# A graph network's set-up: the features' load goes to GpSimd's queue, their largest value is taken earlier, and the verdict goes ahead of the scales

## The reference, cut to what matters

```python
edge_index = jnp.stack([src, dst])
x = _layernorm(x + _L0_gnn_ref(x, edge_index, Wl, bl, Wr, ln_w, ln_b))   # 4 layers: mean over neighbours, two matmuls, layernorm, relu
x = _layernorm(x + _L1_gnn_ref(x, edge_index, edge_weight, W, b))        # sum over neighbours of a linear map
x = _layernorm(x + _L2_gnn_ref(x, src, dst, Wq, Wk, Wv, Wo, ...))        # attention over the edges, batch norms, feed-forward
x = _layernorm(x + _L3_gnn_ref(x, edge_index, W, b))                     # mean over neighbours and a linear map
```

## Time and profile before

| | us |
|---|---|
| three runs | 1333.36, 1333.84, 1334.45 (median 1333.84) |
| the profiled execution | 1335.18 |
| its span, first to last instruction | 1333.2 |
| end of ScalarE's pass over x, last work of the set-up | 51.96 |
| mean granted TensorE clock, as a share of full speed | 0.833 |
| busy: TensorE / VectorE / ScalarE / GpSimd | 990.6 / 867.2 / 523.6 / 413.0 |

### The profile page before, as it was taken

How to read it: one execution, slowest core, us unless ns; L and a number is a source line. 1 busy time by engine, 2 the same in 40 slices (tenths; PEclk the granted TensorE clock), 3 DMA queues, 4 the chain that set the end, 5 groups by cost and what they waited for, 6 DMA issues and landing times. The chain is left out here.

```text
span 1333.2 us, 18242 instructions
## 1 busy us (share of the span) xinstructions
PE 990.6 (74%) x6074; PEld 622.3 (47%) x6074; DVE 867.2 (65%) x2126; ACT 523.6 (39%) x1007; POOL 413.0 (31%) x516
## 2 busy tenths in 40 slices
PE   1289989999999998894655565656656565557997
PEld 1168845645556454454433343434434333345554
DVE  4879946734434467466377877777877777764343
ACT  1289913111111111112456555556655556424210
POOL 4000000000000000001277777777777777720000
PEclk9999999999999999896865766666666766568999
DMA  6000061000000000000543333333333333319000
GB/s 156 26 1 1 1 211 34 1 9 0 9 1 0 17 16 23 12 1 24 154 123 104 106 106 104 106 105 106 107 105 106 107 105 105 107 44 226 12 24 26
DMA packets 49496, 87.78 MB, mean 66 GB/s; under 512 B 12384, under 2 KB 35315, under 8 KB 49161
## 3 DMA queue, kind: packets, MB, share of 16 engines
q0 software_dynamic: 20608, 55.20, 14.4%
q1 hardware_dynamic: 26312, 29.89, 8.3%
q10 hardware_dynamic: 2492, 1.61, 0.5%
HBM read 70.68 MB, written 15.98 MB: 65 GB/s over the span
## 5 line engine op out<-in xcount | busy, mean ns | idle before, releaser
L1413 POOL DMA_INDIRECT counts_all<-kv_d,counts_all x416 | 394.4, 948 | 154.7 <-issue 145.9
L867 PE MATMUL bank<-counts_all,parts 125*128 (+2 forms) x1750 | 344.4, 355 | 19.5 <-DVE parts L1047 9.7
L867 PEld LDWEIGHTS bank<-counts_all,parts 125*128 125x128 f16 x1750 | 159.8, 98 | 190.9 <-DVE parts L1047 11.0
L1553 PE MATMUL bank<-counts_all 125*128 125x128 f16 x1230 | 133.9, 288 | 83.3 <-ACT counts_all L1619 82.9
L1299 POOL IOTA iota_n<- 128x256 f16 x1 | 0.3, 349 | 562.1 <-POOLq L854 562.1
L1553 PEld LDWEIGHTS bank<-counts_all 125*128 125x128 f16 x1230 | 110.1, 133 | 126.6 <-ACT counts_all L1619 126.3
L1542 PE MATMUL bank<-rel_rows,ident_h 104*128 104x512 f16 x104 | 56.9, 547 | 124.6 <-ACT away L1609 123.9
L1483 DVE TENSOR_TENSOR counts_all<-counts_all,bank 128x512 f32<-128x512 f32 x104 | 71.5, 687 | 117.6 <-DMA counts_all<-kv_d,counts_all 117.6
L1568 PE MATMUL bank<-counts_all,parts 128*128 128x272 f16 x615 | 135.2, 378 | 14.3 <-DVE counts_all L1461 12.1
L670 PE MATMUL bank<-parts 128*125 128x125 f16 x625 | 102.7, 324 | 12.0 <-DVE parts L589 12.0
L1609 ACT ACTIVATE away<-bank,lane_bias 125x512 f16<-125x512 f32 x173 | 110.8, 680 | 1.0 <-PE bank L1542 0.7
(11 more groups left out here) (268 smaller groups left out, 1264.2 us busy)
## 6 DMA issues: line engine op xcount, KB each, us to landing
counts_d<-counts_all SPq DMA_DIRECT2D x1, 6835.9 KB
counts_all<-counts_d SPq DMA_DIRECT2D x1, 6835.9 KB
counts_all<-kv_d,counts_all POOLq DMA_INDIRECT x416
kv_d<-counts_all SPq DMA_DIRECT2D x6, 448.0 KB
q_d<-counts_all SPq DMA_DIRECT2D x1, 1562.5 KB
x<-in_x SPq DMA_DIRECT2D x6, 250.0 KB
out<-parts SPq DMA_DIRECT2D x6, 250.0 KB
inv_deg<-in_x SPq DMA_DIRECT2D x1, 1400.0 KB
```

The costliest lines, as they stand in the source:

```text
L867: last = T.matmul(agg_ps[p][:, 0:w], pin[:, s, part, :], counts[:, s, bass.ds(b * BLK, w)], start=(s + part == 0), stop=(s + part == NT))
L1413: G.indirect_dma_start(out=out_rows, out_offset=None, in_=table_d, in_offset=bass.IndirectOffsetOnAxis(ap=index, axis=0)).then_inc(signal, 16)
L1553: last = T.matmul(pick_ps[n % DEEP][:, k * C:(k + 1) * C], ohT[n % DEEP][:, tile - GTILES[n][0], k, :], Q[:, tile, part, :], start=(tile = ...
```

## The change

- SP no longer loads x. GpSimd issues the same two DMAs, behind all its constants and behind waits for both edge lists, and ahead of its five gathers.
- VectorE takes the largest feature (lines 401 to 404) right behind the chunk starts, ahead of the limits.
- VectorE's verdict, with its wait for `edge_ok_summed`, goes ahead of the copy of the largest feature (line 446) and so ahead of `alpha`. The scaled identities stay behind `alpha`.

TensorE's and ScalarE's lists are as they were.

```diff
--- before.py
+++ after.py
@@ -273,9 +273,6 @@
                     load_rows(sp, dst_rows, dst, dst_in)
                     sp.wait_ge(code_ready, 1)
                     sp.dma_start(code_d[:, 0:LANES].rearrange("(g r) p -> r g p", r=ROWS), code[:, :, :]).then_inc(code_out, 16)
-                    x_tiles = x.rearrange("(t p) c -> p t c", p=TILE)
-                    for rows in SPRAY:
-                        sp.dma_start(xf[rows, :, :], x_tiles[rows, :, :]).then_inc(x_in, 16)
                     sp.wait_ge(dstN_ready, 1)
                     sp.dma_start(dstf_d, dstN[:, :]).then_inc(setup_out, 16)
                     sp.wait_ge(srci_ready, 1)
@@ -338,6 +335,12 @@
                     last.then_inc(limits_ready, 1)
                     iota(iota_kp[:, :, :].rearrange("p (s d) w -> p s d w", d=WN), [[1, NT], [NT, WN], [0, BATCH]], 0, 0)
                     iota(iota_tp[:, :, :], [[1, TILE], [0, BATCH]], 0, 0)
+
+                    pool.wait_ge(dst_in, 48)
+                    pool.wait_ge(src_in, 48)
+                    x_tiles = x.rearrange("(t p) c -> p t c", p=TILE)
+                    for rows in SPRAY:
+                        pool.dma_start(xf[rows, :, :], x_tiles[rows, :, :]).then_inc(x_in, 16)
 
                     pool.wait_ge(code_out, 48)
                     pool.wait_ge(chunk0_ready, 1)
@@ -382,6 +385,10 @@
                     dve.wait_ge(chunk0_counted, 1)
                     V.tensor_scalar(chunk0[:, :], ps[3][0:TILE, 0:WBLK], float(CH - 2), None, ALU.min).then_inc(chunk0_ready, 1)
 
+                    dve.wait_ge(x_in, 32)
+                    st.run(V.tensor_reduce(out=absmax[0:TILE, 0:1], in_=xf[:, :, :], axis=AX.XY, op=ALU.max,
+                                           apply_absolute_value=True))
+                    V.tensor_copy(absmax[:, 1:2], absmax[:, 0:1]).then_inc(absmax_ready, 1)
                     dve.wait_ge(limits_ready, 1)
                     dve.wait_ge(dstN_ready, 1)
                     by_group = lambda tile: tile.rearrange("p (g k) -> p g k", k=GRP)
@@ -397,11 +404,6 @@
                     st.done(V.tensor_scalar(edge_ok[:, 2:3], edge_ok[:, 0:1], 0.0, None, ALU.is_lt))
                     st.run(V.tensor_scalar(edge_ok[:, 3:4], edge_ok[:, 1:2], 0.0, None, ALU.is_ge))
                     st.done(V.tensor_tensor(edge_ok[:, 4:5], edge_ok[:, 2:3], edge_ok[:, 3:4], ALU.add))
-
-                    dve.wait_ge(x_in, 32)
-                    st.run(V.tensor_reduce(out=absmax[0:TILE, 0:1], in_=xf[:, :, :], axis=AX.XY, op=ALU.max,
-                                           apply_absolute_value=True))
-                    V.tensor_copy(absmax[:, 1:2], absmax[:, 0:1]).then_inc(absmax_ready, 1)
 
                     def select(j):
 
@@ -439,9 +441,15 @@
                     st.wait()
                     V.tensor_tensor(edge_ok[:, 5:6], edge_ok[:, 6:7], edge_ok[:, 7:8], ALU.add).then_inc(edge_ok_ready, 1)
 
+                    st.done(V.memset(verdict[:, :], 0.0))
                     st.run(V.tensor_scalar(reach[:, 0:3], bound[:, 0:3], LN_BOUND, None, ALU.mult))
                     st.run(V.tensor_tensor(reach[:, 4:7], reach[:, 0:3], bound[:, 4:7], ALU.add))
                     st.run(V.tensor_copy(bound[:, 1:4], reach[:, 4:7]))
+                    st.wait()
+                    dve.wait_ge(edge_ok_summed, 1)
+                    st.done(V.tensor_scalar(verdict[:, 0:1], ps[3][:, 9:10], float(E), 2.0, ALU.is_lt, ALU.mult))
+                    st.run(V.tensor_scalar(verdict[:, 1:2], ps[3][:, 8:9], 0.5, 2.0, ALU.is_ge, ALU.mult))
+                    V.tensor_copy(flags[:, :], verdict[:, :])
                     dve.wait_ge(absmax_all, 1)
                     st.run(V.tensor_copy(bound[:, 0:1], absmax_r[:, 0:1]))
                     st.run(V.tensor_scalar(bound[:, 0:4], bound[:, 0:4], 1e-30, None, ALU.max))
@@ -450,14 +458,8 @@
                     st.run(V.memset(inv_alpha[:, 4:8], 1.0 / ALPHA_LN))
                     V.reciprocal(alpha[:, :], inv_alpha[:, :]).then_inc(alpha_ready, 1)
 
-                    st.done(V.memset(verdict[:, :], 0.0))
                     for l in range(5):
                         V.tensor_scalar(ident_a[:, l, :], ident[:, 0:TILE], inv_alpha[:, l:l + 1], None, ALU.mult)
-                    st.wait()
-                    dve.wait_ge(edge_ok_summed, 1)
-                    st.done(V.tensor_scalar(verdict[:, 0:1], ps[3][:, 9:10], float(E), 2.0, ALU.is_lt, ALU.mult))
-                    st.run(V.tensor_scalar(verdict[:, 1:2], ps[3][:, 8:9], 0.5, 2.0, ALU.is_ge, ALU.mult))
-                    V.tensor_copy(flags[:, :], verdict[:, :])
 
                 @block.tensor
                 def _(pe):
```

## The result

The change makes the kernel a little slower. 20 runs of each: 1334.10 us before (median), 1336.42 after (1334.65 to 1338.38), a ratio of **1.0019 [1.0012, 1.0026]**. One run of before took 1906.18 us and is left out of the ratio; without it the median of before is 1333.97 and the difference some 2.5 us. The ratio is just inside the 0.2% within which the prediction called two times the same. The forecast was 1330.8.

A forecast was written before the change was run, and what follows sets the result against it. The set-up was taken as a serial prelude bounding the run through x's landing, reduce, selections, decode, alpha and ScalarE's pass. Minus 3.5 us for an earlier decode, plus 0.5 for the verdict, gave 1330.8 us from 1333.84; range 1328 to 1341.

The forecast's parts named there:

- The last rows land 2.5 us later: Set-up, x's load: after GpSimd's issue ends at 18.9, x is there at 21.4, 8.6 us sooner.
- no change: x comes no sooner: Rival, set-up: DMA engines are the limit, x lands at 26.4 to 28, run 1334.3 to 1335.9; chance 0.23.
- The issue on GpSimd: Set-up: issuing x's two DMAs costs GpSimd 9.0 us, from 9.9 to 18.9; bounds 6.60 to 23 or 30 us.
- GpSimd's issue is the new bound: Rival, set-up: an issue of 23 to 30 us delays x, run 1343.4 to 1350.5; chance 0.23.
- The limits behind the reduce: VectorE's set-up: reduce ends at 25.0, limits at 28.5, so selections may start 5.1 us sooner than 33.59.
- The gathers: GpSimd's set-up: start at 18.9, fourth issued at 23.6, landing 10.1 us later at 33.7; decode at 35.5, 3.5 us sooner.
- The weights: TensorE's set-up: weights land at 29.11 and their turning until 31.5 fits before the last turn of selected codes.
- the verdict's 0.53 us: VectorE's set-up: verdict ahead of alpha delays the largest feature's copy from 47.94 to about 48.47; bounds 0.25 to 0.8 us.
- `ended` beside GpSimd's issue: VectorE's set-up comparisons, 10.92 to 12.18: taken as nothing; upper bound a wait until 18.9, 8.0 us later.
- The hold-up of a GpSimd DMA by VectorE's fast modes: Set-up, cited rule: x would wait for the casts and `ended`, making the sum about 1.7 us worse; not counted.
- a microsecond off its last chain is a microsecond off the run: Whole set-up: a serial prelude every engine waits for, so its gain should reach the run's end in full.

The follow-up runs named there:

- a1: Kernel before with only x's two DMAs moved to GpSimd's queue, VectorE's order unchanged: 1333.61 us against 1333.81, ratio 1.0002.
- a4: Changed kernel with the six loads of weights and layernorm rows held until x has landed: 1334.60 us, ratio 1.0007.
- c1: a4 with x issued by SP at the same moment and SP's code store moved to ScalarE's queue: 1330.52 us against 1333.31, ratio 0.9971.
- b1: a2 with x on SP's queue right behind the destination list, ahead of SP's wait for the codes: 1327.94 us, ratio 0.9951.
- b3: b1 with the three 103-row transfers cut into 96 and 7 rows: 1320.65 us against 1333.31, ratio 0.9902.
- a2: Kernel before with x reduced ahead of the limits, x still on SP's queue: 1337.02 us, ratio 1.0026.
- a3: Kernel before with only the verdict moved ahead of alpha: 1334.92 us, ratio 1.0011.
- b2: Changed kernel with x issued by GpSimd first of all, without waiting for the edge lists: 1332.36 us, ratio 0.9989.
- a5: Changed kernel with the verdict put back behind alpha: 1336.06 us against 1334.04, ratio 1.0015.
- b4: Changed kernel with the three 103-row transfers cut into 96 and 7 rows: 1332.51 us against 1334.04, ratio 0.999.
- b5: b3 with GpSimd's memsets for the limits moved behind the chunk starts and the reduce behind the limits again: 1321.42 us against 1334.04, ratio 0.9907.

## Why the prediction was wrong, step by step

**The step that failed: "The last rows land 2.5 us later, the time from issue to landing of a transfer with little beside it: x is there at 21.4".** x landed at 28.22, 15.1 us after GpSimd's issue had ended. The 2.5 us belong to a transfer of 220 KB by SP alone; x is 1.6 MB, beside weights, code stores and gathers. The trace of before had the same transfer's own duration: issued at 11.4, there at 30.00, 18.6 us. From 9.9 that gives 28.5. Counted from the end of the issue, as the prediction does, the 2.5 us came out as 15.1; counted from its start, as here, x took 17.8 us in after and 17.6 in a1. With x late the gain went: the limits, put behind the reduce, cost more than x won. What share of the 15.1 is the company and what the queue is known only in part: some 1.5 us are the weights (a4).

**The rival that happened is "no change: x comes no sooner".** It set x at 26.4 to 28 and the run at 1334.3 to 1335.9; x was at 28.22 and the run at 1336.42. With x at 28.22 its own working gives 1.7 us for the limits and 0.5 for the verdict, the 2.2 of the profile. The measured time lies inside the stated 1328 to 1341, but by this rival and not by the forecast's own working. The cause given there, that the shared engines are the limit, fits a1, where x took as long on either queue. It is not all: the company of the weights costs 1.5 us (a4), and with the weights out of the way the request on SP's queue landed 6.2 us sooner (c1), in a pair that differs in more than the queue. The rule of the Trainium skill that was cited with that rival (DMA: Bandwidth & Descriptors, "Rules for kernel authors": another issuing engine buys no bandwidth) pointed the right way. The trace agrees for x itself, 17.6 us against 18.6 (a1); the weights beside it were 6.7 us later, so the moves together got slower.

**Right in kind, wrong in size:**

- *The issue on GpSimd* was put at 9.0 us with bounds from 6.6 up; it took 2.69 (0.92 for 325 rows, 1.77 for 2,800). The lower bound, SP's time, was no bound: SP took 6.60 us for it before, 3.93 in c1, 9.49 in b1 and 4.60 in b3, so its issue goes by what else is in flight; a full queue would do that, and no run shows it by itself. GpSimd was free at 13.1, and the rival "GpSimd's issue is the new bound" had nothing to stand on.
- *The limits behind the reduce*: the prediction let them follow an early x without a gap, and so it is in b3 (16.51, right behind the reduce). With x late they are all on the path (a2: 3.24 us; after: 3.45 less the 1.78 by which x was sooner).
- *The gathers* were not late: the first at 17.89 (18.9 predicted), their landing 9.9 to 12.1 us after issue (10.1 taken), and no wait for them in after.
- *The weights* were said to fit before the last turn, at 31.5. They land at 35.06, turned by 37.46. In after that just fits, since the decode is late too; in a1 it is the end.

**Right:** the verdict's 0.53 us (0.60 measured, inside its bounds of 0.25 and 0.8), shown alone in a3. `ended` beside GpSimd's issue costs 2.09 us instead of 1.26, far from the upper bound of 8.0, and off the path, since the gathers waited for the code stores until 17.89. The hold-up of a GpSimd DMA by VectorE's fast modes, which the prediction cites from the Trainium skill (SBUF — State Buffer, "Summary: rules for kernel authors"), is not seen in the issue's 2.69 us; that the 3 us to the first packet hold some of it is not excluded by any run.

The set-up's 2.20 us came to some 2.5 in the runs, as "a microsecond off its last chain is a microsecond off the run" has it; b3's 12.6 came to 12.7.

## What to carry to other kernels

Before you price the landing of a moved transfer, look for that transfer's own duration in the trace, at its own size and in its own company, and only then for a lone one; and ask whom its packets will crowd out. Putting a consumer ahead of work that filled its wait pays only if the data are really sooner, and costs nearly the filler's whole length if not (a2). Where a semaphore comes late while the DMA engines trickle, look for one transfer on one engine: cutting three transfers of 103 rows was worth some 6 to 7 us here (b3 against b1), as much as x's better place on SP's queue (b1 against before).

## What the runs showed of the hardware

- GpSimd's queue gave its first packets of x 3 us after the start of the issue (10.44 to 13.5; 2.3 in b2), moved them in packets of 4 KB at some 235 GB/s (0.47 MB in 2 us, a4), and ScalarE's packets had 5.9% beside it (after, 16 to 18 us); SP's queue moved 0.53 MB in 2 us (c1).
- From the start of its issue to the last landing, x took 17.6 to 17.9 us on GpSimd's queue and 18.6 on SP's beside weights, code stores and gathers (a1, after, a5; before); 16.2 and 10.5 with the weights held back (a4; c1); 15.1 and 14.6 from the program's start, beside the edge lists (b2; b1); and 10.6 on SP's queue with the 103-row transfers cut (b3).
- Issuing 3,125 rows cost GpSimd 2.4 to 2.7 us (after, b2, b4), less than SP's 3.9 (c1) and 6.6.
- ScalarE's DMA issues can stretch: in after, beside x on GpSimd's queue, the last load of the layernorm rows took 3.39 us to issue, in b3 0.45.
- VectorE's casts of 104x512 take 0.43 us, and 1.51 and 1.34 beside GpSimd's constants (b5, b3).
